# A gated delta-rule layer: the first addition of each block goes from VectorE to GpSimd

## What is computed

```python
def step(S, xs):
    q_t, k_t, v_t, a_t, b_t = xs
    Sk = jnp.einsum('bhvk,bhk->bhv', S, k_t)
    S = a_t[..., None] * S - (b_t[..., None] * (Sk - v_t))[..., None] * k_t[:, :, None, :]
    o_t = jnp.einsum('bhvk,bhk->bhv', S, q_t)
    return (S, o_t)
```

## Time and profile before

| | |
|---|---|
| runs shown | 2372.58 us median of 3 (2368.91 to 2380.48) |
| profiled execution | 2377.0 us, of which the span is 2375.3 us |
| busy, share of the span | PE 87%, PEld 66%, DVE 80%, ACT 52%, POOL 22% |
| granted TensorE clock, mean | 0.92 |
| chain that ended last | PE 49%, DVE 27%, waits within the chain ("issue") 14%, ACT 7% |

### The profile page before, as it was taken

The page is one execution under the profiler, slowest core; times in us unless marked ns, Lnnn a source line. Parts: engine busy times, 40 slices in busy tenths (PEclk is TensorE's granted clock), DMA queues, the critical chain, the costliest instruction groups (busy, mean ns, idle before and its releaser), DMA issues.

```text
span 2375.3 us, 61546 instructions
## 1 busy us (share of the span) xinstructions
PE 2071.1 (87%) x21890; PEld 1575.9 (66%) x21890; DVE 1897.3 (80%) x4382; ACT 1239.1 (52%) x2692; POOL 522.0 (22%) x577
## 2 busy tenths in 40 slices
PE   6999999999994788888888888888887887866999
PEld 4444788888884667667667766666766766742666
DVE  4222699999995788988888988888988988977776
ACT  4000577777772556555555655655655545523332
POOL 0000044444442112221221212222221211221000
PEclk9999999999996899999898989989998988877999
DMA  7000177777779566666666566566666556566440
GB/s 267 9 9 9 62 255 255 255 255 255 264 264 347 182 235 205 214 200 224 208 202 229 188 213 224 192 212 225 205 212 216 194 171 198 187 227 265 178 160 19
DMA packets 229473, 468.45 MB, mean 197 GB/s; under 512 B 48432, under 2 KB 172328, under 8 KB 199640
## 3 DMA queue, kind: packets, MB, share of 16 engines
q1 hardware_dynamic: 222920, 450.91, 54.8%
q10 hardware_dynamic: 6240, 13.86, 1.6%
q0 software_dynamic: 48, 0.16, 0.0%
HBM read 316.36 MB, written 149.57 MB: 196 GB/s over the span
## 4 chain that ended last, share of the span: by engine, by line
PE 49%; DVE 27%; issue 14%; ACT 7%; DMA 2%; DVEq 1%; ACTq 1%; POOL 0%; POOLq 0%; SPq 0%
DVE arena L1081 10%; PE PS L1520 8%; PE PS L1680 5%; PE PS L1596 4%; PE PS L1534 4%; PE PS L1506 4%; PE PS L1387 3%; PE PS L1460 3%; DVE arena L1172 3%; PE PS L1559 3%; ACT arena L856 2%; PE PS L1547 2%; DVE arena L1187 2%; DVE arena L1180 2%; PE PS L1410 2%
## 5 line engine op out<-in xcount | busy, mean ns | idle before, releaser
L1410 PE MATMUL PS<-arena 128*128 x2048 | 463.7, 386 | 1.8 <-DVEq L1066 1.0
L1081 DVE SCALAR_TENSOR_TENSOR arena<-PS,SM,arena 128x256 f32<-128x256 f32 x1152 | 452.9, 478 | 15.5 <-ACT arena L725 15.5
L1410 PEld LDWEIGHTS PS<-arena 128*128 128x128 f32 x2048 | 383.4, 188 | 82.1 <-DVE arena L1081 6.5
L1520 PE MATMUL PS<-arena 128*128 128x128 f32 x1920 | 317.4, 315 | 39.2 <-ACT arena L864 37.5
L1520 PEld LDWEIGHTS PS<-arena 128*128 128x128 f32 x1920 | 267.6, 216 | 77.8 <-ACT arena L864 56.4
L856 ACT ACTIVATE arena<-arena 128x128 f32<-128x128 f32 x960 | 306.8, 396 | 0.0
L631 POOL TENSOR_TENSOR arena<-arena 128x256 f32<-128x256 f32 x128 | 114.6, 895 | 873.2 <-DVE arena L1187 873.2
L725 ACT ACTIVATE arena<-PS,SM 128x256 f32<-128x256 f32 x384 | 209.8, 565 | 88.9 <-PE PS L1410 84.1
L1506 PE MATMUL PS<-ident,arena 128*128 128x128 f32 x960 | 172.7, 309 | 28.3 <-ACT arena L856 27.1
L1126 DVE TENSOR_TENSOR arena<-arena,PS 128x512 f32<-128x512 f32 x192 | 127.5, 685 | 75.4 <-PE PS L1559 71.6
L873 ACT COPY arena<-PS 128x256 f32<-128x256 f32 x240 | 89.6, 373 | 187.2 <-PE PS L1520 184.3
(11 more groups left out here) (135 smaller groups left out, 3170.9 us busy)
## 6 DMA issues: line engine op xcount, KB each, us to landing
arena<-g_d SPq DMA_DIRECT2D x126, 1024.0 KB, 5.6
arena<-vas_d SPq DMA_DIRECT2D x124, 384.0 KB, 3.3
vas_d<-arena SPq DMA_DIRECT2D x32, 1024.0 KB, 11.4
kq_d<-arena SPq DMA_DIRECT2D x8, 4096.0 KB, 11.5
arena<-kq_d SPq DMA_DIRECT2D x14, 2048.0 KB, 8.2
arena<-beta_d SPq DMA_DIRECT2D x8, 2048.0 KB, 9.2
kb_d<-arena SPq DMA_DIRECT2D x8, 2048.0 KB, 10.3
vas_d<-arena SPq DMA_DIRECT2D x8, 2048.0 KB, 12.5
```

Source lines behind the costliest of these rows:

```text
L1081: nc.vector.scalar_tensor_tensor(acc, raw[:, :, i:i + PT_], CW[:, w, i, hh:hh + 1], acc, ALU.mult, ALU.add).then_inc(job_free if i == TAPS ...
L1410: ins = mm(dst.rearrange("p (b n) -> p b n", b=B), W4[:, w, kt, DH * h:DH * (h + 1)], XNT[:, kt, :, bass.ds(c * PT_ + (HALO - halo), halo ...
L1520: ins = mm(bank(7)[:, 128 * gi:128 * (gi + 1)].rearrange("v (l x) -> v l x", l=NB), STR[:, s % 2, gi, :], KQ[d][:, :, p0:p0 + 2].rearrange ...
```

## The change

Block m's `add(0)` is no longer an instruction of VectorE. GpSimd gets it as `first_add`, with the same two inputs and the same output. It stands in GpSimd's list between the two multiplications of block m - 1's outputs and their subtraction (for block 0: ahead of that chunk's first outputs), and waits until the first `level_sub` for this block is done (block 0: until the ninth `head_sub`). `level_sub` no longer waits for `v_add`; `weigh(0)` still does, which now means for GpSimd. The subtraction of the outputs has lost its own wait for `v_add` and stands right behind `first_add`.

```diff
+                def first_add(m):
+
+                    pool.wait_ge(vas_in[m % 4], n * 32 + (16 * (m // 4) + 16))
+                    pool.wait_ge(corr_sub, n * N_SUB + (9 if m == 0 else SUB_AT[m - 1] + 1))
+                    w0 = Xc[:, m, :, 0, 0]
+                    tt(w0, VAS[:, m % 4, 1, :, 0], w0, ALU.add).then_inc(v_add, 1)
+
                 def outputs(m):
...
                     tt(ov, VAS[:, m % 4, 0], Xc[:, m, :, 1, :], ALU.mult).then_inc(o_step, 1)
                     if m % 2 == 0:
                         pool.wait_ge(nested, n * 7 + (m + 1))
-                    if m < NB - 1 or nxt:
-                        pool.wait_ge(v_add, (n * NB + m + 1) * BL + 1)
+                    if m < NB - 1:
+                        first_add(m + 1)
                     pool.wait_ge(o_step, k + 2)
                     tt(ov, OT, ov, ALU.subtract).then_inc(o_step, 1)
...
                     if m == 0:
-                        pool.wait_ge(vas_in[0], n * 32 + 16)
+                        first_add(0)
                         pool.wait_ge(gb_in[0], n * 64 + 16)
...
                     dve.wait_ge(corr_full, n * 9 + 2 + m + 1)
                     dve.wait_ge(nested, n * 7 + NEST_BEFORE[m])
-                    if k == 0:
-                        dve.wait_ge(v_add, (n * NB + m + 1) * BL + 1)
                     tt(dst, dst, src, ALU.subtract).then_inc(corr_sub, 1)
...
                     def add(t):
 
-                        if t == 0:
-                            dve.wait_ge(vas_in[sl], n * 32 + (16 * (m // 4) + 16))
-                            if m == 0:
-                                dve.wait_ge(x_read, 1 + n * 16)
-                            else:
-                                dve.wait_ge(nested, n * 7 + NEST_BEFORE[m - 1])
-                        else:
-                            dve.wait_ge(x_dec, k3 + t)
+                        dve.wait_ge(x_dec, k3 + t)
                         tt(W[:, :, t], V[:, :, t], W[:, :, t], ALU.add).then_inc(v_add, 1)
...
-                    add(0)
                     if m == 0:
```

More of the change, by code:

```diff
@@ L1113, in head_sub @@
                     if b == 0:
-                        dve.wait_ge(v_add, n * NB * BL + 1)
+                        dve.wait_ge(x_read, 1 + n * 16)
                     tt(dst, dst, src, ALU.subtract).then_inc(corr_sub, 1)
@@ L1169, in dec @@
                         else:
+                            dve.wait_ge(vas_in[sl], n * 32 + (16 * (m // 4) + 16))
                             dve.wait_ge(corr_sub, n * N_SUB + (9 if m == 0 else SUB_AT[m - 1] + 1))
```

## The result

The changed kernel takes 2456.82 us (median of 4, 2451.85 to 2462.19) against 2375.31 us: a ratio of 1.0328 (95% interval 1.0297 to 1.0358), 78 us slower by the ratio (81.5 by the medians). The direction was forecast; 2404 us and the range up to 2432 us were far too low.

What follows compares the result with a forecast made beforehand. No engine alone was taken to bound the kernel; the chain through the recurrence's block heads counted. 18.3 + 14.9 - 7.8 = 25.4 us plus 5.3 us for block 7, together 31 us on 2372.6, gave 2404 us; range 2385 to 2432.

Steps and rivals of the forecast that it cites:

- The exclusion: VectorE instructions with two SBUF inputs and GpSimd instructions reading SBUF: one waits for the other's whole instruction.
- its literal reading: Exclusion without 0.14 us of overlap: 1.10 and 0.59 us per head, sum 44 us instead of 31.
- Its prices: Delay at a block's start (head): 0.83 us with one level subtraction, 0.45 us with two.
- Block 0: Its addition runs beside the tenth PSUM subtraction, no GpSimd subtraction behind it: nothing either way.
- the prediction's own chain: Chain that ended last, 763 to 2172 us: 59 of 128 blocks' heads on it, 22 single, 33 double.
- The gain of 7.8 us: add(0) off VectorE in the 26 blocks where it lies on the chain, 0.30 us each.
- Of the heads off the chain, most are covered: TensorE there is late by 1 to 3 us with its own reads; only block 7 adds 5.3 us.
- rival 1: All delays pass through, since late state additions make TensorE's cover vanish: up to 57 us, 2430 us; 13%.
- The upper bound: Every head of blocks 1 to 7 passes its delay on, less 18.0 us for additions: 57 us.
- The late `o_ready`: GpSimd's signal to SyncE's store and loads comes 1.0 to 1.3 us later; counted as nothing.

Runs made afterwards that it cites:

- no_add: sub_ahead with each block's first addition left out, a nop that only signals in its place; 2374.38 us, ratio 0.9993 to the kernel before.
- sub_in_head: Kernel before, add(0) still on VectorE, but GpSimd's output subtraction waits for the next block's first level_sub; 2443.21 us, ratio 1.0256.
- pad_head: Kernel before plus a redundant VectorE multiplication ahead of weigh(0) in blocks 1 to 7, GpSimd untouched; 2446.56 us, ratio 1.0281.
- pad_off: As pad_head, but with the redundant multiplications in blocks 1, 6 and 7 only; 2398.97 us, ratio 1.0114 to the kernel before.
- late_ready: Kernel before, arithmetic unchanged, but GpSimd signals o_ready of blocks 0 to 6 only after the next block's sub(0); 2392.68 us, ratio 1.0055.
- sub_ahead: Changed kernel with GpSimd's output subtraction back ahead of first_add, beside level_sub; 2403.34 us, ratio 1.0093 to the kernel before.

## Why the prediction was right in its direction and wrong in its size

**The exclusion: right.** VectorE operations with both inputs in SBUF and GpSimd's run in turns, those with an input from PSUM run beside them; the durations of both engines show it. "SBUF — State Buffer" of the Trainium skill, section "Who interferes with whom", holds here; its literal reading gave 1.10 and 0.59 us for the heads, the measured ones are 0.92 and 0.54.

**Its prices: slightly low.** 0.83 and 0.45 us were worked out, 0.92 and 0.54 measured. GpSimd's strided 128x64 addition takes 0.43 us undisturbed, not the 0.32 us of the earlier trace rows, a multiplication of other operands; with 0.43 us the prediction's own working gives 0.94 and 0.56. Block 0 was put at nothing and costs 0.13 us. On the prediction's own chain that is 22 x 0.92 + 33 x 0.54 - 7.8 = 30 us instead of 25: not the reason.

**The gain of 7.8 us: not seen.** no_add has no first addition anywhere and is not measurably faster. Its heads in blocks 3 and 5 hold up to 6 us of delay of their own, so a gain of a few us is neither shown nor excluded: the interval's 7 us and these 6 make about 13 us the most that a free offload was worth.

**The step that failed: "Of the heads off the chain, most are covered".** By the prediction's terms, before the 7.8 us are taken off, blocks 1 and 2 were to cost 8 us, blocks 3 to 5 21 us, and blocks 6, 7 and 0 9 us. In the profiled execution they grew by 7, 34 and 36 us. So the cover held in blocks 1 and 2. It did not hold in blocks 3 to 5, nor in blocks 6 and 7, where 12 us of delay cost 39 and 35 us in sub_in_head and pad_head, and 20 us in pad_off, for which the count gave 4 us in all. The start of TensorE's transposes behind VectorE's copy was taken as cover, a microsecond or more in blocks 1, 3 and 6. It was a snapshot: my reading is that a late head also makes the state additions late, then ScalarE's scaling, then the reads that made TensorE look late. The prediction named this as rival 1, with 13%; at 2430 us it was nearer than the forecast, but it was given less weight and is too low as well. That this is the way it takes was not shown apart.

**The upper bound failed too.** "Every head passes its delay on" gave 57 us, and was called the upper end. pad_head shows a loss of 67 us from 45 us of delay. The prediction has no term for TensorE's clock. In the changed kernel five of eleven blocks 6 ran at 0.67 or 0.68 where none did before, and the blocks 7 behind them last 2.8 us longer than the others: 5 x 2.8 = 14 us as an estimate, of the 22 us by which its blocks 7 grew. Why a late head brings these falls about was not shown. The late `o_ready` (13 us by late_ready alone) was put at nothing. How the 78 us divide between the delay, the clock and `o_ready` stays open.

**The parts of the change.** The addition alone costs 29 us (between no_add and sub_ahead; sub_ahead as a whole loses 22), the subtraction that it pushed into the head, with the later `o_ready`, 61 us (sub_in_head); sub_ahead and sub_in_head together lose 83 us against 78.

## What to carry to other kernels

An operation handed from VectorE to GpSimd is not beside VectorE unless VectorE then reads PSUM: look for what else on GpSimd the move pushes along, here a subtraction that had run beside a PSUM read and cost more than the operation moved. Where two engines take turns in a loop-carried dependence, don't take a delay as covered because the chain of one execution passes beside it: here a pure delay of 45 us cost 67. Compare the length of each block before and after, to see where a delay is covered and where it grows. A redundant instruction of the right length on the same spot measures such a price before anything is redesigned.

## What the runs showed of the hardware

In this kernel a fall of TensorE's granted clock was paid for where its work was next waited for, not where it happened: in the changed kernel a block 6 at 0.68 lasts about as long as one at 1.00 (10.80 and 10.45 us), and the block 7 behind it lasts 12.9 us instead of 10.1. And idle time filled with work can win: matmuls that nobody reads made the changed kernel 20 us or more faster and the one before 28 us slower.
